# A dynamic 3x3 convolution after a group norm: raw x into the convolution, statistics shared with ScalarE

## What is computed

```python
def _gn(v, G=32, eps=1e-05):       # 32 groups of one channel each
    m = mean(g); s = var(g)
    return (g - m) / sqrt(s + eps)

xn = _gn(x)
avg = xn.mean(axis=(2, 3))
wk = sigmoid(avg @ w1.T + b1)      # one 3x3 kernel per image and channel
y = depthwise_conv(xn, wk, padding=1) + conv_bias
x = x + (xn - y) * fscale * xn + y
```

## Time and profile before

| | |
|---|---|
| time, median of 3 runs (lowest to highest) | 265.19 us (264.78 to 266.9) |
| span of the profiled execution | 260.2 us (its own time is not given beside it) |
| TensorE busy | 241.6 us, 93% |
| VectorE busy | 232.6 us, 89% |
| GpSimd busy | 225.0 us, 86% |
| ScalarE busy | 210.6 us, 81% |
| DMA | 77.75 MB, 299 GB/s |

### The profile page before, as it was taken

One profiled execution on the slowest core, in us unless ns is written; L12 is line 12 of the kernel. 1 busy time (PEld: TensorE's weight loads), 2 busy tenths in 40 slices (PEclk: granted clock), 3 DMA queues, 4 the chain that ended last, 5 costly groups with the idle time before them and its releaser, 6 DMA issues.

```text
span 260.2 us, 9778 instructions
## 1 busy us (share of the span) xinstructions
PE 241.6 (93%) x3906; PEld 189.5 (73%) x3906; DVE 232.6 (89%) x558; ACT 210.6 (81%) x388; POOL 225.0 (86%) x254
## 2 busy tenths in 40 slices
PE   4899989899899999999999999999999999999991
PEld 3577657658687887878787877878787878888770
DVE  3899999799999999999999999999999998746555
ACT  2177998797988989897989989898979989899510
POOL 1331889599999999999999999999999999999982
PEclk9999999999999999999999999999999999999999
DMA  7999931993989989798979799897989742444476
GB/s 252 414 428 422 412 130 72 339 395 122 341 326 362 345 319 374 264 390 300 347 326 362 292 345 383 295 375 273 362 333 355 296 204 118 184 184 184 185 302 245
DMA packets 10990, 77.75 MB, mean 299 GB/s; under 512 B 1344, under 2 KB 1472, under 8 KB 3264
## 3 DMA queue, kind: packets, MB, share of 16 engines
q1 hardware_dynamic: 10944, 77.12, 77.7%
HBM read 39.37 MB, written 37.75 MB: 296 GB/s over the span
## 4 chain that ended last, share of the span: by engine, by line
PE 56%; DVE 25%; issue 11%; POOL 3%; DMA 2%; ACT 1%; SPq 0%; DVEq 0%; ACTq 0%; POOLq 0%
PE conv_ps L433 36%; PE conv_ps L439 12%; DVE outs L614 10%; DVE pieces L542 9%; DVE taps L559 4%; PE dyn_ps L417 3%; PE dyn_ps L425 2%; DMA xs<-x 2%; POOL outs L893 1%; PE conv_ps L497 1%; DVE taps L566 1%; DVE row_stats L548 1%; POOL inv_std L862 1%; ACT xs L735 1%; DVE outs L624 1%
## 5 line engine op out<-in xcount | busy, mean ns | idle before, releaser
L433 PE MATMUL conv_ps<-xs,taps 64*64 64x448 f32 x1536 | 219.9, 547 | 5.6 <-DVE outs L614 5.2
L893 POOL TENSOR_TENSOR outs<-outs,linear 128x1152 f32<-128x1152 f32 x63 | 165.5, 2645 | 1.3 <-DVE outs L614 1.2
L614 DVE SCALAR_TENSOR_TENSOR outs<-xs,beta,conv_ps 128x576 f32<-128x576 f32 x128 | 102.8, 804 | 18.5 <-PE conv_ps L433 18.2
L433 PEld LDWEIGHTS conv_ps<-xs,taps 64*64 64x64 f32 x1536 | 101.4, 132 | 24.3 <-issue 13.0
L439 PE MATMUL conv_ps<-xs,taps 64*64 64x128 f32 x1536 | 114.0, 271 | 0.0
L771 ACT ACTIVATE linear<-xs,slope 128x576 f32<-128x576 f32 x128 | 109.1, 856 | 2.9 <-POOL outs L893 2.9
L542 DVE BATCH_NORM_STATS2 pieces<-xs 128x6 f32<-128x64 f32 (+1 forms) x256 | 102.6, 448 | 4.8 <-DMA xs<-x 4.8
L439 PEld LDWEIGHTS conv_ps<-xs,taps 64*64 64x64 f32 x1536 | 93.5, 132 | 8.7 <-issue 2.6
L735 ACT ACTIVATE xs<-xs,shift 128x594 f32<-128x594 f32 x128 | 99.5, 780 | 0.0
L862 POOL TENSOR_TENSOR inv_std<-numbers,minus_half 128x8 f32<-128x8 f32 x16 | 26.4, 1648 | 4.3 <-ACT dev_mean L741 4.3
L559 DVE TENSOR_TENSOR taps<-dyn_ps,tap 128x1512 f32<-128x1512 f32 (+1 forms) x19 | 27.8, 1473 | 0.0
(11 more groups left out here) (67 smaller groups left out, 143.1 us busy)
## 6 DMA issues: line engine op xcount, KB each, us to landing
xs<-x SPq DMA_DIRECT2D x30, 1188.0 KB, 11.2
out<-outs SPq DMA_DIRECT2D x30, 1152.0 KB, 5.2
xs<-x SPq DMA_DIRECT2D x8, 297.0 KB, 4.9
out<-outs SPq DMA_DIRECT2D x3, 576.0 KB, 3.4
out<-outs SPq DMA_DIRECT2D x2, 288.0 KB, 2.6
cst<-const SPq DMA_DIRECT2D x1, 275.5 KB, 5.3
w1s<-w1r SPq DMA_DIRECT2D x1, 144.0 KB, 5.1
gates<-gate SPq DMA_DIRECT2D x1, 8.0 KB, 5.6
```

The lines of the kernel that those rows point to most:

```text
L433: return nc.tensor.matmul(tile(i, g, taken)[:, START:BANK], taps[given, i % 2, at:at + HALF], xs[given, i % XBUFS, g, 0:PAIRED, 1 + shift: ...
L614: nc.vector.scalar_tensor_tensor(out=outs[:, i % OBUFS, g].rearrange("p (k w) -> p k w", w=COLS), in0=xs[:, i % XBUFS, g, :, 1:1 + COLS], ...
L893: nc.gpsimd.tensor_tensor(tile, tile, linear[:, PAIR * k:PAIR * (k + 1)].rearrange("p g n -> p (g n)"), ALU.add).then_inc(out_ready, 1)
```

## The change

The convolution reads x as it was loaded; ScalarE no longer centres it. What the mean adds to the convolution, a constant per channel (the sum of the taps that reach into the rows and columns at hand, times the mean), goes into scale and offset of the linear pass. For that VectorE has new small steps: `signed_taps`, `reach_sums`, `drift` and `slopes`, which now sets `gain_ready`, and `deviations` and `average_columns`, which GpSimd did. Their constants and results lie partly in PSUM. ScalarE takes the statistics of the 512-column pieces of tiles 1, 3, 5 and 7: `piece_mean` and `piece_square`, an activation each with a summed output, one after each linear pass (some two in the first image). GpSimd's `scales` has other small operations; its sums stay, and the last two tiles of the last image are still added by VectorE, now out of PSUM (`add_kept`). The order of the first loads, and the places of the small matmuls and of ScalarE's small steps, are changed. The core of the diff:

```diff
-            load_first()
+            load_first(0, 4)
             sp.dma_start(gates[:].rearrange("p a g -> p (a g)"), gate).then_inc(gates_loaded, 16)
+            load_first(4, 6)
             sp.dma_start(cst[:], const).then_inc(consts_loaded, 16)
+            load_first(6, FIRST_LOADS)
...
-                sp.wait_ge(last_ready, k + 1)
+                sp.wait_ge(product_ready, GROUPS * B - PAIR + k + 1)
...
+                pe.wait_ge(gain_ready, j)
...
-            MEAN = {1: (0, 1), 2: (0, 12), 3: (1, 11)}
-            SPREAD = {1: (0, 4), 2: (0, 15), 3: (1, 14)}
-            AVERAGES = {1: (0, 9), 2: (1, 7)}
-            DYNAMICS = {1: (0, 11), 2: (1, 9)}
+            MEAN = {1: (0, 1), 2: (0, 10)}
+            SPREAD = {1: (0, 4), 2: (0, 14)}
+            AVERAGES = {1: (0, 7), 2: (1, 5)}
+            DYNAMICS = {1: (0, 9), 2: (1, 7)}
...
-                    mean = MEAN.get(j, (j - 2, 9))
-                    spread = SPREAD.get(j, (j - 2, 13))
-                    dynamics = DYNAMICS.get(j, (j - 1, 5))
-                    if (i, at) == AVERAGES.get(j, (j - 1, 3)):
+                    mean = MEAN.get(j, (j - 2, 8))
+                    spread = SPREAD.get(j, (j - 2, 12))
+                    dynamics = DYNAMICS.get(j, (j - 1, 6))
+                    if (i, at) == AVERAGES.get(j, (j - 1, 4)):
...
-                pe.wait_ge(centred_ready, n + 1)
+                if g == 0:
+                    pe.wait_ge(margins_ready, 2 * (i + 1))
...
-                    ins = nc.vector.bn_stats(pieces[:, j % 2, g, k, :], xs[:, j % XBUFS, g, a:b, 1:1 + COLS])
+                    if k == 0 or g not in SCALAR_GROUPS:
+                        ins = nc.vector.bn_stats(pieces[:, j % 2, g, k, :], xs[:, j % XBUFS, g, a:b, 1:1 + COLS])
...
+                dve.wait_ge(piece_squares, len(SCALAR_GROUPS))
...
+            def deviations(j):
+                dve.wait_ge(zstats_done, 2 * j + 1)
+                dve.wait_ge(r_ready, j + 1)
+                nc.vector.tensor_tensor(avg[:], zstats_ps[:, 0:GROUPS], inv_std[:, j % 2], ALU.mult).then_inc(avg_ready, 1)
+
+            def average_columns(j):
+                dve.wait_ge(avg_ready, j + 1)
                 nc.vector.tensor_tensor(avg_cols[:, 0:TAPS * C].rearrange("p (a g) -> p a g", g=GROUPS),
-                                        const_of("spread")[:, 0:TAPS * C].rearrange("p (a g) -> p a g", g=GROUPS),
+                                        spread_ps.rearrange("p (a g) -> p a g", g=GROUPS),
                                         avg[:].unsqueeze(1).to_broadcast([PARTS, TAPS * SLOTS, GROUPS]),
                                         ALU.mult).then_inc(avg_cols_ready, 1)
 
-            def product(i, g):
+            def signed_taps(j):
+                dve.wait_ge(tap_ready, j + 1)
+                nc.vector.tensor_tensor(signed[:], tap[:], reach_ps.unsqueeze(1).to_broadcast([PARTS, GROUPS, SETS]),
+                                        ALU.mult).then_inc(signed_ready, 1)
+
+            def reach_sums(j):
+                dve.wait_ge(signed_ready, j + 1)
+                nc.vector.tensor_reduce(reached_ps, signed[:], AX_X, ALU.add).then_inc(reached_ready, 1)
+
+            def drift(j):
+                dve.wait_ge(reached_ready, j + 1)
+                dve.wait_ge(offsets_ready, j + 1)
+                nc.vector.tensor_tensor(drift_ps, offsets[:, j % 2], reached_ps.unsqueeze(1).to_broadcast([PARTS, 2, GROUPS]),
+                                        ALU.mult).then_inc(drift_ready, 1)
+
+            def slopes(j):
+                dve.wait_ge(drift_ready, j + 1)
+                nc.vector.tensor_tensor(slope[:, j % SCALES], bases[:, j % 2], drift_ps, ALU.add).then_inc(gain_ready, 1)
...
+            def add_kept(i, g):
+                n = GROUPS * i + g
+                dve.wait_ge(kept_ready, g - (GROUPS - PAIR) + 1)
+                dve.wait_ge(linear_ready, n + 1)
+                nc.vector.tensor_tensor(outs[:, i % OBUFS, g], conv_ps[:, n % CONV_TILES, START:END], linear[:, g],
+                                        ALU.add).then_inc(product_ready, 1)
...
+            signed_taps(0)
             rows(1)
-            first_matrices(1, PAIRS)
-            for g in range(3):
+            first_matrices(1, 2)
+            reach_sums(0)
+            first_matrices(2, 3)
+            drift(0)
+            first_matrices(3, PAIRS)
+            slopes(0)
...
                     product(i, 0)
-                    bn_ahead(i + 2, AHEAD + 1, GROUPS)
+                    if stats:
+                        rows(i + 2)
                     product(i, 1)
                     bn_ahead(i + 3, 0, 1)
-                    if stats:
-                        rows(i + 2)
                     product(i, 2)
-                    bn_ahead(i + 3, 1, 2)
+                    bn_ahead(i + 3, 2, 3)
                     product(i, 3)
-                    bn_ahead(i + 3, 2, 3)
+                    bn_ahead(i + 3, 5, 7)
                     product(i, 4)
                     if nxt:
+                        signed_taps(i + 1)
                         matrices(i + 1)
-                    bn_ahead(i + 3, 3, 4)
+                        reach_sums(i + 1)
                     product(i, 5)
-                    bn_ahead(i + 3, 4, 5)
-                    product(i, 6)
-                    bn_ahead(i + 3, 5, AHEAD)
+                    if nxt:
+                        drift(i + 1)
+                    bn_ahead(i + 3, 4)
+                    if nxt:
+                        slopes(i + 1)
+                    product(i, 6, stays=i == B - 1)
                     if i == B - 1:
-                        add_last(GROUPS - 2)
-                    product(i, 7)
-            add_last(GROUPS - 1)
+                        add_kept(i, 6)
+                    if stats:
+                        deviations(i + 2)
+                    product(i, 7, stays=i == B - 1)
+                    bn_ahead(i + 3, 6)
+                    if i == B - 1:
+                        add_kept(i, 7)
+                    if stats:
+                        average_columns(i + 2)
...
+            def piece_mean(j, g):
                 wait_for_x(act, j, g)
-                whole = xs[:, j % XBUFS, g].rearrange("p k w -> p (k w)")
-                nc.scalar.activation(whole, whole, ACT.Identity, bias=shift[:, j % 2, 1, g:g + 1]).then_inc(centred_ready, 1)
+                if j < 2:
+                    act.wait_ge(tuples_set, 2)
+                at_least(act, rows_done, j - 1)
+                k = len(SCALAR_GROUPS) * j + SCALAR_GROUPS.index(g)
+                at_least(act, piece_means, k - 1)
+                nc.scalar.activation(spare_means[:, k % 2].rearrange("p (k w) -> p k w", w=COLS), xs[:, j % XBUFS, g, 1:BLOCKS, 1:1 + COLS],
+                                     ACT.Identity, scale=1.0 / PIECE,
+                                     accum_out=pieces[:, j % 2, g, 1, 1:2]).then_inc(piece_means, 1)
+
+            def piece_square(j, g):
+                k = len(SCALAR_GROUPS) * j + SCALAR_GROUPS.index(g)
+                act.wait_ge(piece_means, k + 1)
+                at_least(act, piece_squares, k - 1)
+                nc.scalar.activation(spare_squares[:, k % 2].rearrange("p (k w) -> p k w", w=COLS), xs[:, j % XBUFS, g, 1:BLOCKS, 1:1 + COLS],
+                                     ACT.Square, bias=pieces[:, j % 2, g, 1, 1:2], scale=-1.0,
+                                     accum_out=pieces[:, j % 2, g, 1, 2:3]).then_inc(piece_squares, 1)
...
+            more_statistics(8)
             negative_mean(0)
             fill_margins(0)
-            centre(0, 0)
+            turn_weights()
             copy_stats(0)
-            for g in range(1, 5):
-                centre(0, g)
+            more_statistics(4)
             copy_averages(0)
-            centre(0, 5)
+            more_statistics(1)
             sigmoid(0)
-            centre(0, 6)
+            more_statistics(3)
             count(1)
-            centre(0, 7)
+            more_statistics(2)
...
-            SIGMOID = {1: (0, 6), 2: (1, 6)}
-            MEAN = {1: (0, 0), 2: (0, 7), 3: (1, 7)}
+            SIGMOID = {1: (0, 5)}
+            MEAN = {1: (0, 0), 2: (0, 7)}
+            MORE = {(0, 0): 2, (0, 1): 2, (0, 2): 2}
             for i in range(B):
-                nxt = i + 1 < B
                 for g in range(GROUPS):
                     for j in range(i + 1, min(i + 3, B)):
                         if (i, g) == COPY_STATS.get(j, (j - 1, 0)):
                             copy_stats(j)
-                        if (i, g) == COPY_AVERAGES.get(j, (j - 1, 3)):
+                        if (i, g) == COPY_AVERAGES.get(j, (j - 1, 4)):
                             copy_averages(j)
-                        if (i, g) == COUNT.get(j, (j - 2, 4)):
+                        if (i, g) == (j - 2, 3):
                             count(j)
-                        if (i, g) == SIGMOID.get(j, (j - 1, 5)):
+                        if (i, g) == SIGMOID.get(j, (j - 1, 6)):
```

(22 more changed lines are left out.)

150 lines of the change are left out of this document (90 added, 60 removed).

## The result

The changed kernel takes 310.6 us (median of four runs, 310.18 to 315.68) against 265.0 us before: a ratio of 1.173, 95% interval [1.167, 1.179]. The profiled execution's span is 309.0 us (before: 260.2), its mean granted clock 0.936. So it is slower, inside the range, and 14.6 us above the 296 that was predicted.

A forecast was written before the change was run, and what follows sets the result against it. VectorE was taken to bound the kernel at 14.44 us an image, replaced by a 16.70 us loop: +31.2 by product(12,4), +32.0 after image 13, end -1.05, so +31.0; span 291.2, plus 5.0, gives 296 us, range 268 to 312.

The forecast's parts named there:

- The loop: Product 4 through VectorE's slopes, ScalarE's copy of averages and TensorE's dynamics to the next product 4: 16.70 us against 14.44; 0.60.
- VectorE's leg: Part of the loop on VectorE, from product(i,4) to the end of slopes: 4.54 us.
- ScalarE's with the hand-overs: Part of the loop on ScalarE, linear passes, statistics, count and averages' copy: 6.47 us, plus 0.18 for two hand-overs.
- The 5.0 us that the sum put between span and time: Runs' median of 265.19 lay 5.0 us above the earlier span of 260.2; kept, so span 291.2 became 296.
- The clock: Rival: TensorE's 2.6 us gap brings 1.2 GHz for one tile an image, 18 us more, 314; chance 0.06.
- likeliest case: The new loop decides, with TensorE standing about 2.6 us in each image: 296 us; chance 0.60.
- read-out: Reading out the summed output of ScalarE's means and squares: taken at 0.11 us each, between 0 and 0.25.
- The start: Opening images: ScalarE's statistics delay the first count from 10.85 to 12.95 us; product(2,4) at 74.1, +8.6 on 65.47.
- Image 13: No statistics for group 4 on VectorE and one fewer on ScalarE, so 15.3 us.
- The end: Last image: tile 6's new sum reads its product from PSUM and no longer holds product 7; gain of 1.05 us.
- GpSimd and TensorE as next bounds: Engines behind VectorE: GpSimd's cycle about 14.55 us an image after the change, TensorE's own pace about 14.0.
- the relief: Rival: VectorE's unloading arrives and images take TensorE's 14.0 us, 10 x 0.44 + 1.05 less, 260; chance 0.14.

The follow-up runs named there:

- copy3: Changed kernel with ScalarE's copy of the averages one place earlier in its queue, ahead of linear pass 3, from image 3 on; 274.7 us.
- early: Changed kernel with VectorE's reach_sums, drift and slopes moved right behind signed_taps, ahead of the matrices and product 5; 275.8 us.
- noconst: Changed kernel with the constant part left out of the linear pass from image 2 on, so it need not wait for slopes; 269.7 us.
- dvestats: Changed kernel with the statistics of all eight groups given back to VectorE, the constant part staying in the linear pass; 272.5 us.
- warm: Changed kernel with six TensorE matmuls of constants ahead of each image's dynamic sums from image 3 on, filling the stand; 296.9 us.
- copy2: Changed kernel with ScalarE's copy of the averages two places earlier in its queue, ahead of linear pass 2, from image 3 on; 271.7 us.

## Why the prediction was right, and where it was not

**The loop.** Right, and nearly to the term: VectorE's leg 4.43 us (4.54 predicted), ScalarE's with the hand-overs 6.70 (6.65), TensorE's 5.44 (5.51), together 16.57 (16.70). copy3, early, noconst and dvestats each cut it at another place and each brings back 35 to 41 us. With the clock held up, warm takes 296.9 us beside the predicted 296. That they meet so closely is luck in part: ten loops are 2.2 us shorter than predicted (16.48 against 16.70) and image 14 is 2.3 longer, since warm's matmuls run there too. The 5.0 us that the sum put between span and time is no constant either; it is 1.9 in after (310.93 against 309.0).

**The clock.** This is the step that failed. It stood as a rival with 0.06 and a price of 18 us on top of the loop; it came, at 14 to 16. I had counted the stand itself (2.6 us an image; measured 2.31) and argued that nothing in the run before showed what follows one. That was a reason for a wide chance, not a small one: a stand of that length in each image was a sure part of the likeliest case, so its consequence belonged inside that case. The price was near, but not by its working: it put one tile of every image at half speed, 1.5 us each, where the images of after lose 3.1, 1.7 and 0 in turn. That the range held the time is luck in part: the loop's own range ended at 307, and 312 took in 310.6 only because it reached partly into this rival.

**ScalarE's terms.** A read-out was bounded by 0 and 0.25 and taken at 0.11. Its row is 0.18 long, but the next operation starts 0.10 behind it (80.76 to 80.86). A mean takes 0.52 of queue (80.24 to 80.76), as predicted from the earlier trace rows.

**The start.** First count at 12.67 (12.95 predicted), copy of image 1's variances at 31.02 (30.8), slopes(1) at 46.8 (45.8), product(1,4) at 58.44 (57.4), product(2,4) at 75.00 (74.1; 65.47 in the earlier trace rows): right to about 1 us. The sum left out a low stretch here too: TensorE stands 3.85 us ahead of 34.24, and the granted clock is 0.50 for some 3 us behind it; in the opening of the kernel before it stays at 1.00. Image 13 was predicted at 15.3 and took 17.6 at a clock of 0.90; warm's 16.2 says that some 0.9 of the difference is not clock. Image 14: 13.76 (13.7).

**The end.** The kept products 6 and 7 start at 302.23 and 303.76, 1.53 apart where the earlier trace rows has 2.56: a gain of 1.03 (1.05 predicted).

**GpSimd and TensorE as next bounds.** Both figures were off. noconst runs at 14.35 with all of GpSimd's work, so its cycle of 14.55 was at least 0.2 too long, and the 14.54 of copy2 that seemed to bear it out was, by the rows above, another loop. TensorE's pace was put at 14.0; in noconst it is 14.35. So even the relief, had it arrived, was worth about 1 us in the loop and not the 4.4 in that rival. VectorE was the busiest engine by 0.1 us in 15, GpSimd and TensorE right behind it, and unloading it had next to nothing to give.

## What to carry to other kernels

When a value that was made long ahead is now made late in the step before, follow it once round through the queues of all engines: a queue in order makes everything that stands ahead of the next hand-over part of the loop, whatever the engine's share of busy time. Where the likeliest case has TensorE stand in every step, put the lower clock into that case, as a range, since it did not follow every stand, and give it a price from rows at the lower level. And when a loop is cut, look for the next one by its idle-free stretches before taking the busiest engine as the bound: GpSimd, busy 28.31 of 29.08 us in copy2, was not it.
